# Value products one step behind their scores instead of two, in a two-branch attention kernel

## The reference

```python
xn = _layernorm(x)
s  = attn(xn)           # 16 heads of 8, causal softmax, layer norm with gamma and beta, then Wo
g  = silu(ffn(xn))      # see below
x  = x + s * g
# ffn: rmsnorm, q/k/v (16 query heads, 4 key and value heads), rope, head rmsnorm, causal softmax,
#      gate, Wo, residual, rmsnorm, then the one of 8 experts with the highest logit, residual
scores = jnp.where(causal, einsum('bthd,bshd->bhts', q, k), -inf)
out    = einsum('bhts,bshd->bthd', softmax(scores), v)
```

## Time and profile before

| | |
|---|---|
| median of 3 runs | 809.91 us (808.75 to 810.84) |
| the profiled execution's own time | 805.09 us |
| its span, first to last instruction | 803.4 us |
| busy: PE, ACT, DVE, POOL | 91%, 72%, 70%, 23% |
| chain of work that ended last | PE 72%, DVE 16%, ACT 5% |
| granted TensorE clock, mean | 0.963 |

### The profile page before, as it was taken

How to read it: one execution, slowest core, us unless ns; L and a number is a source line. 1 busy time by engine, 2 the same in 40 slices (tenths; PEclk the granted TensorE clock), 3 DMA queues, 4 the chain that set the end, 5 groups by cost and what they waited for, 6 DMA issues and landing times.

```text
span 803.4 us, 28715 instructions
## 1 busy us (share of the span) xinstructions
PE 729.2 (91%) x12293; PEld 335.4 (42%) x12293; DVE 558.7 (70%) x1488; ACT 579.5 (72%) x682; POOL 185.0 (23%) x356
## 2 busy tenths in 40 slices
PE   1388999999999999999999999989999999999994
PEld 1243343434443444444434444443443434466652
DVE  6977345888787777767688777667878667445436
ACT  1177887778777887888778768766777568787882
POOL 4363113101121102110211031010310334225241
PEclk9589999999999999999999999999999779999997
DMA  4222342042030002000300021000000041445423
GB/s 123 61 64 64 123 139 83 2 79 74 6 118 3 3 2 78 3 3 2 113 10 2 3 80 42 2 3 2 3 3 2 16 159 41 112 115 165 151 61 92
DMA packets 33876, 44.29 MB, mean 55 GB/s; under 512 B 6502, under 2 KB 26342, under 8 KB 33750
## 3 DMA queue, kind: packets, MB, share of 16 engines
q1 hardware_dynamic: 32358, 39.62, 16.8%
q0 software_dynamic: 1248, 2.57, 0.9%
q10 hardware_dynamic: 144, 0.27, 0.1%
HBM read 31.88 MB, written 10.24 MB: 52 GB/s over the span
## 4 chain that ended last, share of the span: by engine, by line
PE 72%; DVE 16%; ACT 5%; issue 5%; DMA 1%; POOL 0%; POOLq 0%; DVEq 0%; ACTq 0%
PE PS L1000 25%; PE PS L978 22%; PE PS L948 14%; PE PS L907 7%; ACT PR L881 5%; DVE MP L1304 4%; DVE PS L1301 2%; PE PS L1010 1%; DVE KA L1225 1%; DVE OT L1324 1%; DMA XN<-in_x 1%; DVE QA L1205 0%; DVE KA L1187 0%; DVE HS L1215 0%; PE PS L1097 0%
## 5 line engine op out<-in xcount | busy, mean ns | idle before, releaser
L881 ACT ACTIVATE PR<-PS 128x1024 f32<-128x1024 f32 (+1 forms) x576 | 531.1, 976 | 126.6 <-PE PS L978 123.9
L978 PE MATMUL PS<-QA,KA 74*32 74x512 bf16 (+3 forms) x5120 | 336.3, 353 | 8.9 <-ACT PR L881 8.3
L1304 DVE TENSOR_REDUCE MP<-PS 128x1 f32<-128x512 f32 x384 | 255.4, 690 | 81.3 <-PE PS L948 80.2
L1000 PE MATMUL PS<-PR,VA 128*18 128x512 f32 (+3 forms) x2560 | 289.5, 535 | 1.4 <-POOL PR L703 0.9
L948 PE MATMUL PS<-KA,QA 72*32 72x512 bf16 (+3 forms) x2560 | 231.2, 354 | 13.0 <-DVE MP L1304 6.8
L703 POOL TENSOR_SCALAR_AFFINE_SELECT PR<-PR 128x256 f32<-128x256 f32 x256 | 103.1, 420 | 447.1 <-ACT PR L881 441.2
L978 PEld LDWEIGHTS PS<-QA,KA 74*32 74x32 bf16 x5120 | 129.3, 97 | 167.5 <-ACT PR L881 74.8
L1301 DVE CUSTOM_DVE_ANT_0 PS<-PS,CON 128x128 f32<-128x128 f32 (+3 forms) x256 | 124.2, 503 | 45.2 <-PE PS L948 42.2
L948 PEld LDWEIGHTS PS<-KA,QA 72*32 72x32 bf16 x2560 | 70.4, 95 | 134.6 <-DVE MP L1304 54.3
L1000 PEld LDWEIGHTS PS<-PR,VA 128*18 128x18 f32 x2560 | 72.3, 99 | 52.5 <-issue 15.4
L1301 DVE DVE_READ_ACCUMULATOR2_ANT MP<- 128x1 f32 x256 | 36.3, 142 | 0.0
(11 more groups left out here) (170 smaller groups left out, 377.8 us busy)
## 6 DMA issues: line engine op xcount, KB each, us to landing
QA<-q_parts SPq DMA_DIRECT2D x96, 96.0 KB
QA<-in_W SPq DMA_DIRECT2D x16, 450.0 KB, 3.3
KA<-k_parts SPq DMA_DIRECT2D x48, 96.0 KB
KA<-in_W SPq DMA_DIRECT2D x7, 450.0 KB
q_parts<-QA SPq DMA_DIRECT2D x4, 384.0 KB, 2.6
q_parts<-KA SPq DMA_DIRECT2D x4, 384.0 KB, 3.8
expert_tokens<-ZERO SPq DMA_DIRECT2D x1, 1483.5 KB, 10.8
QA<-expert_tokens SPq DMA_DIRECT2D x1, 1483.5 KB, 8.6
```

The lines of the kernel that those rows point to most:

```text
L881: act.activation(PR[:, (2 * n + p) % RING, :, 0:w], PS[:, 2 * p:2 * p + 2, 0:w], ACT.Exp)\
L978: last = pe.matmul(PS[r:r + STRIP, hh, start:start + CH - q0], KA[0:ROWS, b, kb // BPC, 0 if ffn else hh, key:key + STRIP], QA[0:ROWS, b, ...
L1000: last = pe.matmul(PS[STRIP * hh:STRIP * hh + 2 * VW, 6, q0:CH], VA[:, slot % 2, kb, hh, VW * (1 - place):VW * (3 - place)], PR[:, (2 * n ...
L1304: dve.reduce_max(top, bank, AX).then_inc(s_mr, 1)
```

## The change

One constant: the value product of a step now stands one step behind its scores.

```diff
@@ -36,7 +36,7 @@
 NT = S // P + NE - 1
 ROW = P + 1
 YRING = 4
-LAG = 2
+LAG = 1
 RING = 7
 NBUF = 3
 STAGED = 4
```

## The result

With values one step behind their scores the kernel takes **815.83 us** (median of 7 runs, 813.29 to 816.16); the kernel before, with four more runs beside it, takes 806.82 us (7 runs, 804.36 to 810.84; the three ahead of the prediction are among them). The ratio is 1.0101, 95% interval 1.0079 to 1.0124: slower. The forecast was 815.9 us, slower. The profiled execution took 816.16 us.

What follows compares the result with a forecast made beforehand. PE, busy 91% of 803.4 us and running its queue in order, was taken as the bound. A +8.4, B +7.2, C -9.9 and D +0.3 gave +6.0 on the median 809.91: 815.9 us, range 805 to 826.

Steps and rivals of the forecast that it cites:

- A: Diagonal steps from step 6: value products wait for POOL's masks; +8.4 us, bounds 0 to 14.
- the pattern of step 145: Two-block diagonal step: its products begin behind POOL's masks at 390.33 instead of 389.85 us; 0.48 us.
- Step 271: Expert stage: POOL issues a DMA first, masks end at 737.57, PE would come at 736.70; 1.02 us.
- B: Start: PE stands 3.2 us for step 2's masks, net 2.2, then half clock costs 5; +7.2 us.
- C: Router: places come earlier, PE's pause becomes 1.05 to 1.2 us, half clock goes; -9.9 us, or -0.6 if it stays.
- D: Bank 7: turns and FFN pieces come one step earlier, some meetings part, others form; +0.3 us, bounds -2.8 and +3.4.
- T8: Bank 7: this transpose of the shift now meets a turn; +1.0 us.
- L and E: Bank 7: both fall in one step twice, PE's second transposes wait for ACT, some 1.05 each; +2.1 us.
- the second (no early fall): Start: the clock does not fall, leaving 2.2 us there; +1.0 in all, 810.9 us; chance 0.20.
- the first (half clock stays): Router: half clock near 632 us stays; 825.8 us; chance 0.17.
- The third: Whole kernel: PE's slack, its waits for maxima and DVE, takes the new waits up; -4.6, 805.3 us; chance 0.15.
- The fourth: Many short pauses lower the clock once more, say at step 30; +6.0 + 9.3, 825.2 us; chance 0.08.

Runs made afterwards that it cites:

- two_block_two: Changed kernel, but values of diagonal steps with two blocks follow by two steps: 809.83 us, ratio 1.0016 to the kernel before.
- ffn_later: Changed kernel with the dense layer, router and places back in the steps of the kernel before: 823.67 us, ratio 1.0194 to the kernel before.
- moe_two: Changed kernel, but values follow by two steps from step 256, layer-norm transposes a step later as before: 811.34 us, ratio 1.0049 to the kernel before.
- no_rewait: Changed kernel without the value product's own wait for the exponentials, except in the last step: 814.33 us, ratio 1.0085 to the kernel before.
- ln_later: Changed kernel with the layer-norm transposes one step later, in the steps they had before: 815.34 us, ratio 1.0091 to the kernel before.
- expert_whole: Changed kernel with both expert-layer products as whole matmuls instead of strips: 814.99 us (2 runs), ratio 1.0092 to the kernel before.
- start_two: Changed kernel, but values follow by two steps up to step 23: 810.76 us, ratio 1.0035 to the kernel before.
- before_again: The kernel before, unchanged, run and profiled again (the second execution): 807.80 us, ratio 1.0005 to the kernel before.

## Why the prediction was right, and where two errors met

The sign and the mechanisms held, and the time came out to 0.1 us. But that figure is better than its working. The forecast was +6.0 us on a median of 809.91, which came from three runs; in the runs beside the changed kernel before has 806.82, so the change cost 9.0 us between the medians, and 8.0 between the two spans of the table (before, second). A base 3 us too high met an effect too small. By terms:

**A, forecast +8.4, measured 6.7.** Beside the 3.36 us of the start, PE's idle time for masks is 8.1 - 3.4 = 4.7 us in 11 pieces, all for two-block steps. That is less than the delay. Idle time is counted from the modelled end of the matmul ahead, and a product that nothing holds starts 0.17 us before that end. So starts have to be compared. Step 55 shows both cases, the product of step 54 without a wait and then that of step 55, behind its masks:

```profile
190.04 0.39 PE L948 MATMUL PS<-KA,QA 72*32 72x512 bf16 x4
190.26 1.03 PE L1000 MATMUL PS<-PR,VA 128*18 128x512 f32 x8
...
190.76 1.68 POOL L703 TENSOR_SCALAR_AFFINE_SELECT PR<-PR 128x256 f32<-128x256 f32 x4 [1.69 <-ACT PR L881]
...
191.89 0.39 PE L948 MATMUL PS<-KA,QA 72*32 72x512 bf16 x4
192.59 1.06 PE L1000 MATMUL PS<-PR,VA 128*18 128x384 f32 x16 [0.31 <-POOL PR L703]
```

The first product starts 0.22 us behind the maxima ahead of it, the second 0.70: 0.48 us late, the forecast's figure, and 0.15 behind the masks' end at 192.44, the forecast's hand-off. Read in this way, the 30 two-block steps from step 11 on are 6.7 us late in all, and the other diagonal steps 0.1 for the forecast's 0.8. two_block_two bears this out: from step 31 to 235 it saved 3.5 us and did one more product (0.85 us), where the delays come to 3.9.

The step that failed is the pattern of step 145, read for a product that moves alone. In the changed kernel it looks like this:

```profile
398.05 1.03 PE L1000 MATMUL PS<-PR,VA 128*18 128x512 f32 x8
...
398.32 1.69 POOL L703 TENSOR_SCALAR_AFFINE_SELECT PR<-PR 128x256 f32<-128x256 f32 x4 [0.51 <-ACT PR L881]
...
399.01 0.66 PE L1010 MATMUL PS<-CON,OT 128*128 128x128 f32 x4
...
400.49 1.04 PE L1000 MATMUL PS<-PR,VA 128*18 128x384 f32 x16
```

The masks end at 400.01, the product comes at 400.49 and waits for nothing. In between stands the turn of the group that ended at step 143: the same change moved it from step 146 to 145, ahead of the product. So it is in steps 109 and 217, which also lie two behind the end of a group: I had moved the products and left the turns where they were. These three were some 1.5 us of the forecast (twice 0.48 and 0.59), most of what is missing. Step 271 cost 0.6 us, not 1.02.

**B, forecast +7.2, measured 6.3, with a second fall of the clock that it did not hold.** The pause is 3.36 for 3.2 us. Step 6 starts 3.2 us later than before, with one product more done (0.85 us), so 2.4 net for the forecast's 2.2; the first stretch of half clock had ended by then. Steps 7 and 8 add 4.0, for the 5 that I had for one long fall. In them lie the wait of 1.02 us for DVE's copy-out and the second stretch, and neither was in the forecast. Five other runs (ffn_later, moe_two, no_rewait, ln_later, expert_whole) have the same start, with the pause of 3.3 to 3.4 us, one stretch of half clock of 6.8 us that begins inside it, and the same pause of 1.02 to 1.03 us in step 7. There the clock stays full behind that pause and steps 7 and 8 add 0.7: step 9 starts 4.6 to 5.8 us late, for 7.2 in the changed kernel's profile, so B is 3.8 to 4.9 net. The mechanism held, the size was met in part by luck. By the Trainium skill (TensorE: Matmul & The Clock Gate, "HAM oscillation — how this bites in real kernels"), whose pause is longer, the clock would not have fallen 1.8 us into one; the row at 52.4 us has it fall there, and the row decides. start_two gives the term back.

**C, forecast -9.9, measured -9.0 against the profile it was read from, -4.3 against the second execution.** Steps 212 to 246, in which both kernels have the same matmuls, take 91.45 us for 100.68 in the first profile and 95.98 in the second; of the difference 0.9 is T13's wait (term D), and the masks of steps 214 and 224 add 0.6. The mechanism is right: the pause is 0.54 us, the clock stays full, and ffn_later brings 1.70 us and half clock back. The size was the wrong part, and the largest error of the sum. I took 20.5 us of half clock as the kernel's own; the same pause of 1.70 us was followed by 6.8 us in before_again and 10.2 in ffn_later. One execution can't say how long a fall lasts.

**D, forecast +0.3, about -1.2 by its waits.** The meetings that part are gone as said (-3.8). T8 costs 0.8 for the 1.0 forecast, L and E 1.8 for 2.1 (1.4 by ln_later's trace). POOL's power ahead of step 272's masks costs nothing, for the 1.0 forecast: they end at 745.90, and the product comes at 746.37 without a wait.

Together 6.7 + 6.3 - 4.3 - 1.2 = 7.5, for the 8.0 between the spans: C came out 5.6 us too small, and A, B and D together 4.1 below their forecasts, so that the sum was nearer than its terms. What no term held, the gaps in the expert steps, is in the unchanged kernel as well: 5.9 of the 9.6 us by which that stage is longer than in the first profile come from there, and 3.6 from the change (87.89 less 84.27), of which A and D name 2.7.

Of the rivals, the second (no early fall) and the first (half clock stays) are ruled out by the rows of the clock. The third, slack that takes the waits up, did not come: PE's waits for maxima (L1304) are 7.4 us, for 6.8 in the first profile. The fourth, a fall at step 30, did not come in this execution; in three variants (ffn_later, ln_later, expert_whole) some 3.3 us of half clock do stand behind the masks of step 29, as in ffn_later:

```profile
125.50:128.80 3.30, 3.30 (x48) 2.42 (x52) 0.00 (x0) 0.00 (x0) 3.30 (x5) 0.50 0.37 118
```

## What to carry to other kernels

When a step of a pipeline is moved, move everything that is counted from it before looking for what comes late: the turn that came along covered three waits. To price a wait, compare starts with a place where nothing waits, since the idle time in brackets left out 0.17 us of each delay here. Before a stretch of half clock or a stage's length is put into a sum, look at a second execution, for here the same program had 20.5 and 6.8 us of the one and 78.3 and 84.3 us of the other. And a setting that is one number for the whole kernel can be right in one stage alone: one step paid from step 172 to 255 and cost everywhere else.

## What the runs showed of the hardware that I had not expected

- Expert steps with 44 matmuls in some 3 us (24 of them strips of 32 columns) run with gaps of about 0.4 us in which PE waits for nothing that the profile shows. With whole matmuls in their place, 26, 32 or 38 matmuls in a step, no gap is left, at 3.35 to 3.39 us a step; without gaps the strips took 3.04.
- The same pause of 1.70 us was followed by half clock of 20.5, 6.8 and 10.2 us in three executions.
- The same short pause is followed by half clock in one execution and not in another: that of 1.02 us in step 7 in one of seven executions (6.8 us), the wait of 0.9 to 1.0 us for step 29's masks in three of seven (3.4 us).
- A product that waits for masks starts 0.14 to 0.15 us after the last select when its queue first passes a wait for exponentials that is already met, and 0.05 us after it without that wait (no_rewait).
